# Attention kernel: the two transposed pieces of a cell back to back, and a step's fill in two parts

## The chip, the cores and the metric

The kernel runs on 1 core of a Trainium2 chip. The metric is device time in microseconds (us). The core's engines are TensorE (PE, its weight loads listed as PEld), VectorE (DVE), ScalarE (ACT), GpSimd (POOL) and SyncE (SP, which issues the DMAs). They run side by side and are ordered by semaphores that the program waits on and increments itself.

## What is computed

One transformer layer for x of shape (2, 1024, 512): attention with 32 query heads and 8 key/value heads of width 128, then a feed-forward layer with 4-bit weights, each with a residual and a layer norm. The part that matters here:

```python
scores = jnp.einsum('bhqd,bhkd->bhqk', q, k) * scale
scores = jnp.where(causal[None, None], scores, -1000000000.0)
attn = jax.nn.softmax(scores, axis=-1)
out = jnp.einsum('bhqk,bhkd->bhqd', attn, v)
out = out.transpose(0, 2, 1, 3).reshape(bsz, q_len, N_HEADS * HEAD_DIM)
return out @ Wo.T
```

Every product is made of three passes over operands that are split in a high and a low part (`PASSES`: high by high, high by low, low by high), so each logical 128x128 by 512 product is three matmuls of 512 columns.

## The kernel before

The program has three stages. A projects keys and values and stores them. B, the attention, takes about 1835 of the 2507 us. C is the feed-forward part. The change touches B alone.

B is a loop of 16 turns, one for each pair of batch and key/value head, of about 114 us each. A turn has 32 steps, one for each cell. Cell c is query tile i = c // 4 (128 queries) of head h = c % 4 in the group of four; its scores have 128 x (i + 1) columns, since the mask is causal. In step s:

- PE multiplies the scores of cell s into `b_sps` (three matmuls, or six from step 16 on), transposes cell s - 3 (`LAG`), and does some fill.
- DVE takes mask and maximum of cell s (L869) and writes it to SBUF (`b_sc`), and ACT makes the exponential of it (L708).
- DVE takes the reciprocal of the sum (L877) and ACT normalises (L714) for cell s - 2.
- The normalised cell s - 3 is transposed by PE in blocks of 128x128 (L1006) into PSUM, `b_tps`. ACT copies the high part of that to `b_pt` (L729, `hi_pt`), then DVE subtracts it for the low part (L887, `lo_pt`).

A cell's transposed blocks come in **pieces** of up to four: cells 0 to 15 have one piece, cells 16 to 31 two (the first has four blocks, the second one to four). There are two `b_tps` buffers, used in turn; from cell 16 on the first piece goes to one and the second to the other. A piece may be written when DVE has subtracted the piece two before it: `transposes` waits for `pt_lo`, beside the normalisation, `norm_done`.

**Fill** is the other work of PE in the turn: 24 jobs in the table FILL, with their earliest steps. They are the products with the values (`pv`), the output projection (`wo`) and the queries of coming steps (`q0`, `q1`), 300 matmuls of 512 columns a turn. Each job writes one of two banks, in turn, and may start when the job before it in that bank has been drained by ACT and DVE. ROOM says how many matmuls a step holds. `cut` divides the fill of a step among its places in the order, by SHARES: SHARES[1] for cells of one piece, SHARES[2] for two. Step 0 does all its fill ahead of its scores.

The order within a step is written by hand, for each engine. `part_of` divides the turn in four: steps 0 to 2, 3 to 15, 16 to 23 and 24 to 31. In steps 0 to 2 the transposed cells are 29, 30 and 31 of the turn before, which have two pieces. PE's orders are PE_ORDER; ACT's and DVE's (ACT_ORDER, DVE_ORDER) have "0" and "1" for the copies and subtractions of the two pieces. An engine works its instructions off in that order, so one that waits holds those behind it. If the shares are used up, a "fill" in the order does nothing:

```python
for job in PE_ORDER[part_of(step)]:
    ...
    elif job == "fill":
        if shares:
            fill(it, turn, shares.pop(0))
    elif job < len(ts):
        transposes(*cell, ts[job])
```

SP loads the keys of a turn at its step 0, after all scores of the turn before (`s_done`), and the other inputs far ahead.

Of the kernel before, what the change touches and what calls it, by code (L numbers as in the profile page):

```python
# [54 lines left out]
def pieces(c):  # L55

    i = c // GQ
    first = c if i < 4 else 16 + 2 * (c - 16)
    out = [(first, 0, min(4, i + 1))]
    if i >= 4:  # L60
        out.append((first + 1, 4, i - 3))
    return out
# [31 lines left out]
def part_of(step):  # L94

    return (step >= LAG) + (step >= 16) + (step >= 24)
# [12 lines left out]
             ("take", "max", "q", 0, 1))  # L109
PE_ORDER = (("scores", "fill", "fill", 0, "fill", 1),  # L110
            ("fill", "scores", 0, "fill", "fill", 1),
            ("scores", "fill", 0, "fill", 1, "fill"),
            ("scores", "fill", 0, "fill", 1, "fill"))

SHARES = ((1,), (0, 1), (1, 1.25, 1))


def products(kind, a):
# [50 lines left out]
def cut(parts, weights):  # L169

    total, shares = sum(b - a for _n, a, b in parts), []
    ends = [round(total * sum(weights[:k]) / sum(weights)) for k in range(len(weights) + 1)]
    for lo, hi in zip(ends, ends[1:]):
        at, share = 0, []
        for place, a, b in parts:
            x, y = max(lo, at), min(hi, at + b - a)
            if x < y:
                share.append((place, a + x - at, a + y - at))
            at += b - a
        shares.append(share)  # L180
    return shares
# [68 lines left out]
def attention(nc, x, xT, wqT, wkrT, wdkT, wupkT, wupvT, woT, cosT, sinT, xs_d, k_d, v_d, y_d):  # L250


    with ExitStack() as ctx:
# [700 lines left out]
        def _(pe):  # L954
# [126 lines left out]
            def turn_of(it, turn):  # L1081
                for step in range(CELLS):
# [5 lines left out]
                    ts = pieces(cell[1]) if cell else []  # L1088
                    shares = cut(parts, SHARES[len(ts)])
                    for job in PE_ORDER[part_of(step)]:  # L1090
# [560 lines left out]
```

## Time and profile before

| | |
|---|---|
| three runs | 2506.01, 2510.23, 2511.68 us; median 2510.23 |
| profiled execution | 2508.73 us, its span 2506.9 |
| DVE, ACT, POOL busy | 57%, 64%, 23% of the span |
| granted TensorE clock | 0.989 of full speed over the span |
| DMA queue q1 | 35.1% of 16 engines' span |

PE is the busiest engine by far, in every slice of the span after the first:

```profile
PE   6999999999999999999999999999999996899998
PEld 5887888888888888887888888888888875677876
DVE  3334666666656666665666666666666665842332
ACT  3223878787777877787777777787877762322211
```

Each digit is the busy share of a fortieth of the span in tenths. The attention loop is slices 4 to 33. A matmul's listed duration is longer than the distance to the next one, since they are pipelined: its end is modelled. So costs of PE's work are read here as distances between starts in the timeline.

### The profile page before, as it was taken

How to read it: one execution, taken by the hardware profiler on the slowest of the kernel's cores; microseconds unless marked ns; L12 is line 12 of the kernel's file. 1: busy time of each engine (PE TensorE's matmuls, PEld its weight loads, DVE VectorE, ACT ScalarE, POOL GpSimd, SP SyncE). 2: the span in 40 equal slices, each digit the busy share in tenths (PEclk: the TensorE clock that was granted, in tenths of full speed). 3: DMA queues.
4: the chain of work that ended last, by engine and by line, in shares of the span. 5: the costliest groups of instructions: out<-in, count | busy, mean ns of one | idle time of the engine just before them, and what ended most of it. 6: DMA issues, size and time to landing. Idle time of an engine off the chain costs nothing. (4 is left out here: it accounts for less than half of the span.)

```text
span 2506.9 us, 40455 instructions
## 1 busy us (share of the span) xinstructions
PE 2409.5 (96%) x12016; PEld 1996.6 (80%) x12016; DVE 1430.8 (57%) x3325; ACT 1598.3 (64%) x3204; POOL 573.1 (23%) x443
## 2 busy tenths in 40 slices
PE   6999999999999999999999999999999996899998
PEld 5887888888888888887888888888888875677876
DVE  3334666666656666665666666666666665842332
ACT  3223878787777877787777777787877762322211
POOL 4002323132231313132232313231322202300000
PEclk9999999999999999999999999999999998999999
DMA  8657333234242323233242423232332316520110
GB/s 292 225 209 287 123 100 116 95 106 129 80 161 90 126 84 126 100 109 113 93 155 69 152 79 130 90 123 92 109 125 84 122 39 185 155 75 34 50 34 17
DMA packets 109681, 293.33 MB, mean 117 GB/s; under 512 B 10689, under 2 KB 27585, under 8 KB 99969
## 3 DMA queue, kind: packets, MB, share of 16 engines
q1 hardware_dynamic: 109632, 292.73, 35.1%
q8 instruction: 25, 0.41, 0.1%
q14 instruction: 24, 0.19, 0.0%
HBM read 208.80 MB, written 88.08 MB: 118 GB/s over the span
## 5 line engine op out<-in xcount | busy, mean ns | idle before, releaser
L887 DVE TENSOR_TENSOR b_pt<-b_tps,b_pt 128x512 fp32r<-128x512 f32 (+3 forms) x768 | 427.5, 557 | 333.5 <-ACT b_pt L729 332.5
L714 ACT ACTIVATE b_sc<-b_sc,b_rinv 128x896 f32<-128x896 f32 (+7 forms) x512 | 397.3, 776 | 308.7 <-DVE b_rinv L877 303.6
L245 PE MATMUL b_sps<-b_kt,b_qs 128*128 128x512 f32 (+4 forms) x2304 | 501.6, 344 | 10.4 <-DMA b_kt<-k_d 10.4
L245 PE MATMUL b_ps<-b_pt,b_vt 128*128 128x512 f32 x1728 | 480.0, 404 | 2.5 <-DVE b_ys L898 2.5
L245 PE MATMUL b_ps<-b_xs,b_wq 128*128 128x512 f32 x1536 | 445.9, 410 | 16.9 <-DVE b_qf L851 13.2
L245 PEld LDWEIGHTS b_sps<-b_kt,b_qs 128*128 128x128 f32 x2304 | 404.1, 188 | 70.9 <-issue 16.5
L245 PE MATMUL b_ps<-b_wo,b_ot 128*128 128x512 f32 x1536 | 424.0, 406 | 1.8 <-DVE b_ys L898 0.6
L729 ACT ACTIVATE b_pt<-b_tps 128x512 fp32r<-128x512 f32 (+3 forms) x768 | 365.0, 475 | 64.1 <-PE b_tps L1006 63.4
L708 ACT ACTIVATE b_sc<-b_sc,b_nmax 128x896 f32<-128x896 f32 (+7 forms) x512 | 392.5, 767 | 1.0 <-DVE b_nmax L869 1.0
L869 DVE CUSTOM_DVE_ANT_0 b_sc<-b_sps,b_mask 128x896 f32<-128x896 f32 (+7 forms) x512 | 381.2, 745 | 0.6 <-issue 0.3
L1006 PE MATMUL b_tps<-b_ident,b_sc 128*128 128x128 f32 x2304 | 374.8, 273 | 2.4 <-DVE b_pt L887 1.6
L245 PEld LDWEIGHTS b_ps<-b_pt,b_vt 128*128 128x128 f32 x1728 | 310.8, 189 | 56.8 <-DVE b_ys L898 3.0
L1006 PEld LDWEIGHTS b_tps<-b_ident,b_sc 128*128 128x128 f32 x2304 | 289.9, 140 | 77.7 <-issue 8.3
L245 PEld LDWEIGHTS b_ps<-b_xs,b_wq 128*128 128x128 f32 x1536 | 272.4, 190 | 73.5 <-DVE b_qf L851 27.3
L245 PEld LDWEIGHTS b_ps<-b_wo,b_ot 128*128 128x128 f32 x1536 | 270.6, 189 | 48.6 <-DVE b_qf L851 4.1
L577 POOL TENSOR_TENSOR b_sw<-b_sw,b_sin 128x512 f32<-128x512 f32 x128 | 165.0, 1289 | 502.4 <-ACT b_sw L682 502.4
L581 POOL TENSOR_TENSOR b_qs<-b_qf,b_qs 128x512 fp32r<-128x512 f32 x124 | 160.4, 1294 | 480.9 <-ACT b_qs L688 480.9
L877 DVE RECIPROCAL b_rinv<-b_rsum 128x1 f32<-128x1 f32 x512 | 81.7, 160 | 246.6 <-PE b_sps L245 233.8
L245 PE MATMUL c_a<-c_xs,c_w 128*128 (+3 forms) x528 | 135.5, 407 | 8.2 <-DVE c_hb L1437 4.2
L1545 PE MATMUL c_y<-c_w,c_hs 128*128 128x512 f32 (+1 forms) x528 | 132.4, 400 | 7.1 <-DVE c_hs L1443 6.9
L590 POOL TENSOR_TENSOR b_wo<-b_wraw,b_wo 128x512 fp32r<-128x512 f32 x64 | 82.4, 1288 | 242.5 <-ACT b_wo L702 242.5
L851 DVE TENSOR_TENSOR b_qf<-b_ps,b_cos 128x512 f32<-128x512 f32 x128 | 88.5, 692 | 86.1 <-POOL b_qs L581 44.0
(127 smaller groups left out, 2315.1 us busy)
## 6 DMA issues: line engine op xcount, KB each, us to landing
b_xs<-xs_d SPq DMA_DIRECT2D x32, 2048.0 KB, 9.2
b_ys<-y_d SPq DMA_DIRECT2D x128, 256.0 KB, 2.6
y_d<-b_ys SPq DMA_DIRECT2D x128, 256.0 KB, 2.4
k_d<-a_ks SPq DMA_DIRECT2D x32, 512.0 KB, 4.1
v_d<-a_vs SPq DMA_DIRECT2D x32, 512.0 KB, 2.9
b_kt<-k_d SPq DMA_DIRECT2D x64, 256.0 KB, 4.5
b_vt<-v_d SPq DMA_DIRECT2D x16, 1024.0 KB, 4.8
b_wraw<-in_wqT SPq DMA_DIRECT2D x64, 256.0 KB, 2.7
```

The source lines that it names most:

```text
L245: ins = nc.tensor.matmul(out, *every[n], start=(n == 0), stop=(n == len(every) - 1))
L577: nc.gpsimd.tensor_tensor(sw[:], sw[:], sinq[:, blk * TB:blk * TB + TB], ALU.mult).then_inc(sin_done, 1)
L581: nc.gpsimd.tensor_tensor(qs[:, blk, h, LO], qf[:], qs[:, blk, h, HI], ALU.subtract).then_inc(q_lo, 1)
L590: nc.gpsimd.tensor_tensor(wo[:, h, LO], wraw[:, h % 2], wo[:, h, HI], ALU.subtract).then_inc(w_lo, 1)
L708: nc.scalar.activation(sc[:, slot, 0:w], sc[:, slot, 0:w], ACT.Exp, bias=nmax[:, slot:slot + 1], scale=-1.0, accum_out=rsum[:, slot:slot + ...
L714: nc.scalar.activation(sc[:, slot, 0:w], sc[:, slot, 0:w], ACT.Copy, scale=rinv[:, slot:slot + 1])\
L729: nc.scalar.activation(pt[:, u % PT_UNITS, HI, 0:nj, h * P:(h + 1) * P], tps[n % 2][:, 0:nj], ACT.Copy)\
L851: nc.vector.tensor_tensor(qf[:], bank[bk][:], cosq[:, blk * TB:blk * TB + TB], ALU.mult)\
L869: nc.vector.tensor_tensor_reduce(out=like_banks(sc[:, slot, 0:w], i), in0=both_banks(sps[c % 2], i), in1=like_banks(mask[:, S - w:S], i), ...
L887: nc.vector.tensor_tensor(pt[:, u, LO, 0:nj, h * P:(h + 1) * P], tps[n % 2][:, 0:nj], pt[:, u, HI, 0:nj, h * P:(h + 1) * P], ALU.subtract) ...
L1006: last = nc.tensor.transpose(tps[n % 2][:, j], sc[:, c % S_RING, (j0 + j) * P:(j0 + j + 1) * P], ident[:])
L1545: last = nc.tensor.matmul(yps[t][:], hs[0:w, f % 2, a, t * P:(t + 1) * P], w2[0:w, b, f], start=(f == 0 and k == 0), stop=(f == FT - 1 and ...
```

## The change

The third and fourth order of PE have both pieces of a cell next to each other, with one fill ahead of them and one behind. The fill of a step whose cell has two pieces is divided in two equal shares, where it was in three of 1 : 1.25 : 1.

```diff
@@ -109,10 +109,10 @@
              ("take", "max", "q", 0, 1))
 PE_ORDER = (("scores", "fill", "fill", 0, "fill", 1),
             ("fill", "scores", 0, "fill", "fill", 1),
-            ("scores", "fill", 0, "fill", 1, "fill"),
-            ("scores", "fill", 0, "fill", 1, "fill"))
-
-SHARES = ((1,), (0, 1), (1, 1.25, 1))
+            ("scores", "fill", 0, 1, "fill"),
+            ("scores", "fill", 0, 1, "fill"))
+
+SHARES = ((1,), (0, 1), (1, 1))
```

The orders of ACT and DVE stay, and so do FILL and ROOM: each step holds the same matmuls.

## Rows read from the trace of the kernel before

**Rows 1.** The page: span, and PE's busy time, its share, instructions

```profile
span 2506.9 us, 40455 instructions
...
PE 2409.5 (96%) x12016; PEld 1996.6 (80%) x12016; DVE 1430.8 (57%) x3325; ACT 1598.3 (64%) x3204; POOL 573.1 (23%) x443
```

**Rows 2.** Busy times by stretch: turn 8, then its steps 19 to 31

```profile
1146.22:1260.19 113.97, 112.30 (x590) 94.11 (x588) 71.58 (x176) 89.01 (x185) 30.70 (x24) 1.00 0.33 110
...
1205.19:1256.78 51.59, 51.59 (x273) 43.75 (x272) 33.53 (x72) 39.55 (x74) 10.38 (x9) 1.00 0.18 56
```

**Rows 3.** Groups of instructions: busy, mean ns, idle before, releaser

```profile
L1006 PE MATMUL b_tps<-b_ident,b_sc 128*128 128x128 f32 x2304 | 374.8, 273 | 2.4 <-DVE b_pt L887 1.6
```

**Rows 4.** PE's timeline in step 21 of turn 8: start, us, what

```profile
1212.02 1.09 PE L245 MATMUL b_ps<-b_pt,b_vt 128*128 128x512 f32 x4
1212.95 0.60 PE L1006 MATMUL b_tps<-b_ident,b_sc 128*128 128x128 f32 x4
1213.30 1.18 PE L245 MATMUL b_ps<-b_wo,b_ot 128*128 128x512 f32 x4
1214.32 0.27 PE L1006 MATMUL b_tps<-b_ident,b_sc 128*128 128x128 f32 x1
1214.34 1.17 PE L245 MATMUL b_ps<-b_wo,b_ot 128*128 128x512 f32 x4
```

**Rows 5.** PE's timeline, steps 0 to 4 of turn 8

```profile
1152.30 1.04 PE L1006 MATMUL b_tps<-b_ident,b_sc 128*128 128x128 f32 x8
1153.09 0.60 PE L245 MATMUL b_sps<-b_kt,b_qs 128*128 128x256 f32 x3
...
1155.27 0.60 PE L1006 MATMUL b_tps<-b_ident,b_sc 128*128 128x128 f32 x4
...
1156.52 0.60 PE L245 MATMUL b_sps<-b_kt,b_qs 128*128 128x256 f32 x3
1156.96 1.08 PE L245 MATMUL b_ps<-b_wo,b_ot 128*128 128x512 f32 x4
...
1158.34 0.60 PE L1006 MATMUL b_tps<-b_ident,b_sc 128*128 128x128 f32 x4
...
1159.47 0.60 PE L1006 MATMUL b_tps<-b_ident,b_sc 128*128 128x128 f32 x4
1159.83 0.60 PE L245 MATMUL b_sps<-b_kt,b_qs 128*128 128x256 f32 x3
1160.35 0.33 PE L1006 MATMUL b_tps<-b_ident,b_sc 128*128 128x128 f32 x1
1160.44 1.64 PE L245 MATMUL b_ps<-b_xs,b_wq 128*128 128x512 f32 x6
1161.92 0.52 PE L245 MATMUL b_sps<-b_kt,b_qs 128*128 128x256 f32 x3
```

**Rows 6.** Timelines of PE and DVE, steps 20 and 22 of turn 8

```profile
1209.04 0.60 PE L1006 MATMUL b_tps<-b_ident,b_sc 128*128 128x128 f32 x4
...
1216.41 1.09 PE L245 MATMUL b_ps<-b_wo,b_ot 128*128 128x512 f32 x4
...
1209.46 0.29 DVE L887 TENSOR_TENSOR b_pt<-b_tps,b_pt 128x128 fp32r<-128x128 f32 x1 [0.80 <-ACT b_pt L729]
...
1216.54 0.69 DVE L892 TENSOR_TENSOR b_ot<-b_ps,b_ot 128x512 fp32r<-128x512 f32 x1 [0.20 <-ACT b_ot L736]
```

**Rows 7.** ACT's timeline, steps 1 and 2 of turn 8

```profile
1155.90 0.60 ACT L729 ACTIVATE b_pt<-b_tps 128x512 fp32r<-128x512 f32 x1
...
1157.99 0.58 ACT L729 ACTIVATE b_pt<-b_tps 128x512 fp32r<-128x512 f32 x1
...
1158.98 0.60 ACT L729 ACTIVATE b_pt<-b_tps 128x512 fp32r<-128x512 f32 x1
```

**Rows 8.** DVE's timeline, step 2 of turn 8

```profile
1158.60 0.69 DVE L887 TENSOR_TENSOR b_pt<-b_tps,b_pt 128x512 fp32r<-128x512 f32 x1 [0.75 <-ACT b_pt L729]
...
1159.61 0.69 DVE L887 TENSOR_TENSOR b_pt<-b_tps,b_pt 128x512 fp32r<-128x512 f32 x1
```

**Rows 9.** Waits: who for whom, us in total, times, longest us

```profile
PE b_sps L245 <- DMA b_kt<-k_d: 10.4, 14, 1.6
```

## The prediction

> **What bounds the kernel now.** I read the page's busy times first: TensorE's matmuls are busy 96% of the span, DVE and ACT far less [rows 1]. Then the stage view, for one turn of the attention loop (1146.22 to 1260.19, turn 8 counted from 0) and for its steps 19 to 31. In the turn, matmuls are busy 112.30 of 113.97 us; in steps 19 to 31, busy and stretch are both 51.59 us [rows 2]. So PE sets the time, nothing is waited for in the steps that the change is named after, and 1.67 us a turn are lost elsewhere. In all 2304 transposes PE sat idle 2.4 us [rows 3]. Two questions are left: does PE work become cheaper when transposes are merged, and does the new order make PE wait? For the second I laid PE's timeline beside ACT's and DVE's and asked of each moved group what releases it and who waits for it.
>
> **What really changes.** PE_ORDER changes steps 16 to 31. In steps 16 to 18 the cell has one piece and SHARES[1] stands, so nothing moves. In steps 19 to 31, F T0 F T1 F becomes F T0 T1 F (F: fill, T0 and T1: the two pieces). But SHARES[2] is also used by steps 1 and 2, where the last cells (30 and 31) of the turn before are transposed in the order scores, fill, fill, T0, fill, T1. With two shares the third fill is empty: all fill now runs ahead of T0. Step 0 has no fill left by then; steps 3 to 15 have one piece. No instruction is added or removed on any engine, and no queue of SP or POOL is reordered.
>
> **Term 1, merging in steps 19 to 31.** Take step 21 [rows 4]. Four fills ahead of T0 take 0.93 us (0.2325 each). T0's four transposes take 0.35 to the start of the next fill, and the four fills behind them 1.02, 0.09 more than 0.93. So a group of four costs 0.35 + 0.09 = 0.44, or 0.11 each. The lone T1 behind them starts 0.02 ahead of the next fill and leaves the same tail, 0.11 again. The only run of eight, at step 0, takes 0.79 before the next matmul starts [rows 5], 0.44 more than the run of four: again 0.11 each. Cost is proportional to the count, whatever the grouping. I take zero. Rounding allows 0.02 us either way for each of 13 x 16 = 208 merges: -4 to +4 us.
>
> **Term 2, waits in steps 19 to 31.** T0 moves behind half the fill, up to three matmuls (0.7 us) later, and T1 up to two matmuls earlier, less T0's own shift. T1 needs its PSUM buffer drained by DVE (L887) for the cell before. The tightest is step 20: T0 moves from 1209.04 to about 1209.50 (two fills), T1 to 1209.94 behind it (0.44 for four); DVE frees the buffer at 1209.46 + 0.29 = 1209.75 [rows 6]. It passes by 0.19. Fill jobs that now start before T0 need their bank: in step 22 the query job would start at about 1216.41 + 0.93 = 1217.34, and its bank is drained at 1216.54 + 0.69 = 1217.23 [rows 6], passing by 0.11. Both cost zero; if such a wait does open by 0.2 us in both, it is 0.4 x 16 = 6 us. ACT gets T0 later, but steps 19 to 31 show no PE wait [rows 2], and what ACT makes in a step (the next cell's normalised scores) PE reads in the next step at the earliest.
>
> **Term 3, steps 1 and 2: the loss.** Here ACT and DVE run right behind PE. Today T0 of cell 31 starts at 1158.34 and ends 0.60 later at 1158.94 [rows 5]; ACT's copy starts at 1158.98 [rows 7]; it ends at 1158.98 + 0.60 = 1159.58 and DVE starts at 1159.61, ending at 1160.30 [rows 8]; the one transpose of step 3, which writes the same buffer, starts at 1160.35, and its lead of 0.09 to the next matmul is not that of an unwaited one (0.02) [rows 4, 5]. Its natural start: in step 2 three scores matmuls behind a group of transposes take 0.44 (1156.52 to 1156.96) [rows 5], so 1159.83 + 0.44 = 1160.27. The chain through ACT and DVE already ends last, by 0.08.
> The change puts three more fills ahead of T0 of cell 31: 3 x 0.23 = 0.69, so it starts at 1159.03, if nothing else holds it. ACT then copies at 1159.67, DVE subtracts 1160.30 to 1160.99, and step 3's transpose starts at 1161.04 instead of 1160.35: PE is 0.69 us late.
> Is another path later? In step 1 two fills move ahead of T0 of cell 30, which starts 0.46 later (1155.73, end 1156.33). ACT's copy at 1155.90 [rows 7] started as soon as T0 was there (1155.27 + 0.60), so it moves to 1156.36, and with it ACT's queue behind it: rope's hi part, the normalisation of cell 31, the copy of T1 of cell 30 (1157.99 to 1158.45 [rows 7]), exp. DVE's subtraction for that T1 moves from 1158.60 to 1159.06 and ends at 1159.75 [rows 8]. T1 of cell 31, which needs that buffer, would start at 1159.03 + 0.44 = 1159.47, its place of today [rows 5]; it waits until 1159.80, 0.33 late. That makes step 2 longer by 0.33 to 0.4 and step 3 by the rest: 0.69 is the total, not added to it. ACT is free for T0's copy at 1158.98 + 0.46 = 1159.44, before 1159.67. What ACT and DVE do behind that moves by some 0.4, less than PE, so by step 4 nothing new is late.
> Nothing gives the 0.69 back. PE waits 10.4 us in all for keys [rows 9] at the starts of turns, but that load is issued on the last scores of the turn (s_done), so it moves with PE. What PE waits for in steps 3 to 15 otherwise are drains of a bank (L851 and its like), chains that start at PE's own last matmul of a job and move with it.
> Turns 1 to 15 have such a step 2 and 3: 15 x 0.69 = 10.35. The tail after turn 15 has T0 and T1 without scores; I estimate 0.3 for it, between nothing and one more 0.69. Sum: +10.65 us, with 0 from terms 1 and 2.
> Per-turn bounds: 0.46, if T0 of cell 31 were moved only by what step 1's shift gives, to 0.77, if today's 0.08 of wait came on top. That is +7 to +12 us.
>
> **The time.** The profiled execution took 2508.73 us, of which its span is 2506.9 [rows 1], 1.50 below the median of the runs, 2510.23. Against itself it becomes 2519.4; against the median 2520.9, which I predict.
>
> **The rivals.**
> (a) The forecast: 2520.9, own range 2516 to 2525 (term 3's bounds give 2517 to 2522.5, and some of term 1's come on top). Chance 0.74.
> (b) Slower still: the passes of 0.19 and 0.11 in steps 20 and 22 turn into waits, since ACT's copies of T0 come late and DVE's later work with them, or the merged run costs 0.02 each: +10.65 + 6 = 2527, to 2531 with +4. For: the margins are thin. Against: the copies that free these buffers are released by DVE's maxima today, not by T0. Chance 0.08.
> (c) No change: PE's loss at steps 2 and 3 is given back at the keys' wait of the next turn. 10.4 us over 14 waits is 0.74 each [rows 9], just enough for 0.69. It decides if the load is not on PE's own path; the net is then +0.3, 2510.5. Against: the code's wait on the last scores. Chance 0.12.
> (d) Faster: merged transposes come closer. If the 0.08 to 0.09 behind a group is paid once per step rather than twice, at no longer pitch within, 208 x 0.085 = 17.7 us go: 2510.2 + 10.65 - 17.7 = 2503.2. It needs that a longer run hides its weight loads better; the run of eight at 0.44 for its second four speaks against. Chance 0.06.
> The Trainium skill, "TensorE: Matmul & The Clock Gate", section "Back-to-back issue gap", has a rule on the side of (d): pairs of weight load and matmul of 128 columns sustain about 81 ns each. By it, a run of eight would be near 0.65 us, an estimate; the trace has 0.79 for its starts alone, so here it does not hold, and by it alone the merged runs of 80 transposes a turn would gain an estimated 0.028 us each, 36 us in all. The sum goes by the rows.
>
> **How the numbers follow.** 0.2% (5 us) is about what a measurement of this kernel can tell from no change. Faster by more: (d), 0.06. Within: (c) and a thin lower edge of (a), 0.13. Slower: 0.81. The range for 8 in 10 leaves out (c), (d) and the upper half of (b): 2514.5 to 2527.
>
> **What would show it.** Step 2 of a turn (3.31 us from its scores, 1156.52, to the next, 1159.83 [rows 5]) longer by 0.3 to 0.4; step 3 (1159.83 to 1161.92, 2.09 [rows 5]) longer by 0.3; a PE wait on DVE L887 of some 0.3 to 0.5 us twice a turn, where all turns together have 1.6 now [rows 3]; steps 19 to 31 still 51.6 us, all busy. It is wrong if the step 3 transpose is not behind DVE's subtraction, or if steps 19 to 31 change by over 0.2 us.

## The result

The changed kernel takes 2521.18 us (median of 5 runs, 2517.47 to 2523.64), the kernel before 2507.12 (5 runs, 2504.60 to 2511.68). The ratio is 1.0052, 95% interval 1.0040 to 1.0065: slower by 13 us, between 10 and 16. The forecast was 10.65 us slower, at 2520.9. That the two absolute times lie 0.3 us apart is luck: the forecast stood on a median of 2510.23 us for the kernel before, and with more runs that median is 3.1 us lower.

The first line of the changed kernel's page, to set against [rows 1]:

```profile
span 2520.8 us, 40455 instructions
```

The instructions are the same in number; the span is 13.9 us longer, and matmuls are busy 96% of it as before. Not all of that belongs to the change. Here are the scores' matmuls, the kernel before first, then the changed one: count, ns of one, first and last start.

```profile
L245 PE MATMUL b_sps<-b_kt,b_qs x2304: 274/338/477, 241.3 to 2048.0; 128*128 128x384 f32 x48, 128*128 128x512 f32 x48, 128*128 128x256 f32 x32, 128*128 128x320 f32 x32
```

```profile
L245 PE MATMUL b_sps<-b_kt,b_qs x2304: 274/339/478, 242.8 to 2061.2; 128*128 128x384 f32 x48, 128*128 128x512 f32 x48, 128*128 128x256 f32 x32, 128*128 128x320 f32 x32
```

The attention loop starts 1.5 us later, in a stage that the change doesn't touch. From its first scores to its last it takes 1806.7 us before and 1818.4 after: 11.7 us more. That is the part to explain.

The waits of PE for DVE's subtraction, in all: us, times, longest. It was 1.6 us on the matmuls before [rows 3].

```profile
PEld b_tps L1006 <- DVE b_pt L887: 11.8, 28, 0.5
...
PE b_tps L1006 <- DVE b_pt L887: 8.9, 36, 0.7
```

A weight load stands ahead of each matmul and can show the same wait, so the two lines are not to be added.

**Steps 2 and 3.** PE's timeline of turn 8, from the scores of step 2 to those of step 4. It answers to [rows 5].

```profile
1163.36 0.60 PE L245 MATMUL b_sps<-b_kt,b_qs 128*128 128x256 f32 x3
1163.79 1.09 PE L245 MATMUL b_ps<-b_wo,b_ot 128*128 128x512 f32 x4
1164.72 1.31 PE L245 MATMUL b_ps<-b_xs,b_wq 128*128 128x512 f32 x5
1165.87 0.60 PE L1006 MATMUL b_tps<-b_ident,b_sc 128*128 128x128 f32 x4
1166.62 0.66 PE L1006 MATMUL b_tps<-b_ident,b_sc 128*128 128x128 f32 x4 [0.15 <-DVE b_pt L887]
1167.04 0.60 PE L245 MATMUL b_sps<-b_kt,b_qs 128*128 128x256 f32 x3
1167.88 0.33 PE L1006 MATMUL b_tps<-b_ident,b_sc 128*128 128x128 f32 x1 [0.25 <-DVE b_pt L887]
...
1169.44 0.52 PE L245 MATMUL b_sps<-b_kt,b_qs 128*128 128x256 f32 x3
```

Step 2, counted from its scores to the next, takes 1167.04 - 1163.36 = 3.68 us, where it took 3.31; step 3 takes 2.40, where it took 2.09. Turns 1 to 14 all show this, at 0.66 to 0.70 us for the two together. All nine fills stand ahead of the first piece, and the second piece starts 0.75 after it, not 0.44. ACT's and DVE's timelines of the same stretch tell why (ACT first; these answer to [rows 7, 8]):

```profile
1163.20 0.60 ACT L729 ACTIVATE b_pt<-b_tps 128x512 fp32r<-128x512 f32 x1 [0.44 <-PE b_tps L1006]
...
1166.50 0.60 ACT L729 ACTIVATE b_pt<-b_tps 128x512 fp32r<-128x512 f32 x1 [0.28 <-PE b_tps L1006]
```

```profile
1165.87 0.69 DVE L887 TENSOR_TENSOR b_pt<-b_tps,b_pt 128x512 fp32r<-128x512 f32 x1 [1.19 <-ACT b_pt L729]
...
1167.13 1.50 DVE L887 TENSOR_TENSOR b_pt<-b_tps,b_pt 128x512 fp32r<-128x512 f32 x2 [0.30 <-ACT b_pt L729]
```

ACT waits for the late first pieces of cells 30 and 31 (0.44 and 0.28). DVE's subtraction for the second piece of cell 30 ends at 1165.87 + 0.69 = 1166.56, and PE goes on at 1166.62. DVE's next subtraction starts at 1167.13 and takes about 0.7 of the two listed together: it ends near 1167.82, and step 3's transpose starts at 1167.88.

**Step 22.** It takes 4.61 us, where it took 4.40. The busy times of the step, the kernel before first, then the changed one:

```profile
1215.35:1219.75 4.40, 4.40 (x25) 3.77 (x24) 2.92 (x7) 3.57 (x9) 0.00 (x0) 1.00 0.00 0
```

```profile
1222.94:1227.55 4.61, 4.61 (x25) 3.74 (x23) 2.88 (x7) 3.38 (x7) 0.00 (x0) 1.00 0.00 0
```

PE's timeline in the changed kernel, then the query job's weight loads, then DVE's drain of the bank (the matmuls and the drain answer to [rows 6]):

```profile
1224.01 1.08 PE L245 MATMUL b_ps<-b_wo,b_ot 128*128 128x512 f32 x4
1225.05 0.72 PE L245 MATMUL b_ps<-b_xs,b_wq 128*128 128x512 f32 x2
```

```profile
1225.04 0.30 PEld L245 LDWEIGHTS b_ps<-b_xs,b_wq 128*128 128x128 f32 x2 [0.38 <-issue]
```

```profile
1224.11 0.69 DVE L892 TENSOR_TENSOR b_ot<-b_ps,b_ot 128x512 fp32r<-128x512 f32 x1 [0.20 <-ACT b_ot L736]
```

The query job's first matmul starts 1.04 us after the start of the four projections, not 0.93, and its second 0.33 after it, not 0.23. The group has 0.1 + 0.1 too much. Load and matmul start together, at 1225.04 and 1225.05. The bank was free at 1224.11 + 0.69 = 1224.80.

Turn 0 of the same kernel shows the job without the loss. DVE's drain, the job's loads, its matmuls:

```profile
305.61 0.69 DVE L892 TENSOR_TENSOR b_ot<-b_ps,b_ot 128x512 fp32r<-128x512 f32 x1 [0.20 <-ACT b_ot L736]
```

```profile
306.41 0.41 PEld L245 LDWEIGHTS b_ps<-b_xs,b_wq 128*128 128x128 f32 x2
```

```profile
306.64 0.62 PE L245 MATMUL b_ps<-b_xs,b_wq 128*128 128x512 f32 x2
```

There the drain ends 0.2 us earlier in the step, at 306.30, the load leads its matmul by 0.23, and step 22 takes 4.39. So in turn 8 the unhindered load would stand at about 1224.01 + 0.93 - 0.23 = 1224.71, and the drain is 0.09 late for it. The load then follows the drain by 0.24 (0.23 to 0.24 in each of turns 1 to 14), where the transposes of step 2 followed DVE's subtraction by 0.06. The profile puts the wait down to no engine (`issue`). The code of a query job (`queries`) has three waits in a row ahead of its first matmul, the bank's first, and the trace has instructions of PE's sequencer between the drain and the load. That these waits make up the 0.24 is likely, and not shown by a run.

**The rest.** The stretch that [rows 2] calls steps 19 to 31 ends where the scores of step 31 begin, so it holds steps 19 to 30; step 31 takes 3.41 us in both kernels, all of it busy. The busy times of steps 19 to 30 of turn 8, and of steps 24 to 30, in the changed kernel, after stretch and length:

```profile
1212.76:1264.45 51.69, 51.69 (x274) 44.25 (x272) 33.47 (x72) 39.54 (x72) 10.41 (x9) 1.00 0.18 56
...
1231.35:1264.45 33.10, 33.10 (x173) 28.16 (x171) 21.98 (x45) 26.04 (x46) 7.67 (x6) 1.00 0.12 40
```

Steps 19 to 30 go from 51.59 to 51.69 us [rows 2] though step 22 alone is 0.21 longer: steps 24 to 30 became shorter, 33.24 to 33.10. Turns 0 to 14 all show this 0.15. In turn 15, which has no queries of a next turn among its fill, the same steps are 0.71 us longer: the second piece now waits for DVE's subtraction in steps 25 and 28, 0.40 and 0.37 us, where it waited for nothing before. The view calls the whole stretch busy in both kernels; a wait of this kind between two matmuls is hidden under the modelled end of the one before.

### The profile page after: what moved, and what is told of

It reads as the page before. It is cut to its first block and busy times, and to the rows that moved or that the text cites. A ratio compares the mean times of both kernels' runs of the same rounds, so it can differ in the third digit from the quotient of the medians.

```text
span 2520.8 us, 40455 instructions
## 1 busy us (share of the span) xinstructions
PE 2415.6 (96%) x12016; PEld 2005.6 (80%) x12016; DVE 1428.4 (57%) x3325; ACT 1604.0 (64%) x3204; POOL 573.8 (23%) x443
## 5 line engine op out<-in xcount | busy, mean ns | idle before, releaser
L245 PE MATMUL b_sps<-b_kt,b_qs 128*128 128x512 f32 (+4 forms) x2304 | 501.4, 344 | 10.7 <-DMA b_kt<-k_d 10.7
L245 PE MATMUL b_ps<-b_pt,b_vt 128*128 128x512 f32 x1728 | 460.6, 399 | 2.1 <-DVE b_ys L898 2.0
L245 PE MATMUL b_ps<-b_xs,b_wq 128*128 128x512 f32 x1536 | 429.7, 406 | 16.3 <-DVE b_qf L851 13.2
L245 PE MATMUL b_ps<-b_wo,b_ot 128*128 128x512 f32 x1536 | 413.9, 403 | 1.3
L1006 PE MATMUL b_tps<-b_ident,b_sc 128*128 128x128 f32 x2304 | 340.8, 273 | 9.8 <-DVE b_pt L887 8.9
L1006 PEld LDWEIGHTS b_tps<-b_ident,b_sc 128*128 128x128 f32 x2304 | 277.7, 140 | 65.2 <-DVE b_pt L887 11.8
```

Source lines behind the costliest of these rows:

```text
L245: ins = nc.tensor.matmul(out, *every[n], start=(n == 0), stop=(n == len(every) - 1))
L1006: last = nc.tensor.transpose(tps[n % 2][:, j], sc[:, c % S_RING, (j0 + j) * P:(j0 + j + 1) * P], ident[:])
```

## The experiments

Each is the kernel before, or the changed one, with one part done or undone. All but the last read the shares of a step from a table:

```diff
+SHARES_AT = {...}
-                    shares = cut(parts, SHARES[len(ts)])
+                    shares = cut(parts, SHARES_AT.get(step, SHARES[2]) if len(ts) == 2 else SHARES[len(ts)])
```

with SHARES[2] at (1, 1.25, 1) again. Lines behind it are one higher than in the kernel before. My theory (A) was that the loss lies in steps 2 and 3 and in the bank wait of step 22, and that merging costs nothing. The rival (B) was that the merged order itself costs.

### Late steps alone

```diff
-            ("scores", "fill", 0, "fill", 1, "fill"),
-            ("scores", "fill", 0, "fill", 1, "fill"))
+            ("scores", "fill", 0, 1, "fill"),
+            ("scores", "fill", 0, 1, "fill"))
+SHARES_AT = dict.fromkeys(range(16, 32), (1, 1))
```

> The changed order and two shares in steps 16 to 31 alone; steps 1 and 2 of a turn keep their three shares. Theory A (the loss sits in steps 2 and 3, 0.68 us a turn, and in the bank wait of step 22, 0.22 us a turn; merging itself costs nothing): steps 2 and 3 back at 3.31 and 2.09 us, step 22 still at 4.61, and with the small differences of the other steps about 0.13 us a turn over the kernel before, +2 us in all (ratio 1.0008). Rival B (the merged order bears the loss, and steps 2 and 3 are late only because ACT's and DVE's work of steps 22 to 31 is): steps 2 and 3 stay long, +8 us or more (1.003 and up).

Measured: 2509.39 us against 2507.61, ratio 1.0007 (0.9999 to 1.0016). Its busy times from the scores of step 2 to those of step 4, and of step 22:

```profile
1157.69:1163.10 5.41, 5.41 (x34) 4.53 (x32) 4.15 (x14) 4.68 (x12) 1.30 (x1) 1.00 0.00 0
1216.60:1221.21 4.61, 4.61 (x25) 3.75 (x24) 2.89 (x7) 3.39 (x7) 0.00 (x0) 1.00 0.00 0
```

Steps 2 and 3 are back at 5.41 together (5.40 before), step 22 stays at 4.61. B falls: what the change does in the steps that it is named after bears some 2 of the 13 us, with an interval from nothing to 4.

### Early steps alone

```diff
+SHARES_AT = {1: (1, 1), 2: (1, 1)}
```

> The old order of steps 16 to 31 with three shares; only steps 1 and 2 have two shares, so all their fill stands ahead of the first piece. Theory A: step 2 3.68 us, step 3 2.40 us, all else as in the kernel before: 15 x 0.68 = +10.3 us (ratio 1.0041). Rival B: steps 2 and 3 hardly longer, at most +3 us.

Measured: 2520.94 us against 2507.61, ratio 1.0048 (1.0036 to 1.0060). The point, 12 us, is above the 10.3 of A, and 10.3 lies in the interval. PE's timeline in steps 2 and 3:

```profile
1164.81 0.66 PE L1007 MATMUL b_tps<-b_ident,b_sc 128*128 128x128 f32 x4 [0.16 <-DVE b_pt L888]
...
1166.07 0.33 PE L1007 MATMUL b_tps<-b_ident,b_sc 128*128 128x128 f32 x1 [0.25 <-DVE b_pt L888]
```

The same two waits, with the old order in all late steps. Nearly all of the loss comes from the shares, in steps whose order the diff doesn't show.

### Step 22 mended

```diff
 # late_only, and:
+SHARES_AT[22] = (4, 8)
```

> As late_only, but step 22 has 4 of its 12 fill matmuls ahead of the merged transposes and 8 behind, so that the query job starts behind them. Theory A (its bank is drained too late for the weight load of a first matmul that stands ahead of the transposes): step 22 falls from 4.61 to 4.38 to 4.40 us, and the whole to 0.09 us a turn under the kernel before, -1.5 us (ratio 0.9994). Rival C (step 22 is longer because the transposes or ACT's copies are late there, not for the bank): step 22 stays at 4.5 us or above.

Measured: 2506.21 us against 2507.61, ratio 0.9996 (0.9988 to 1.0005). Its step 22, busy times, and the transposes and queries in its timeline:

```profile
1214.27:1218.66 4.39, 4.39 (x25) 3.82 (x24) 2.90 (x7) 3.56 (x9) 0.00 (x0) 1.00 0.00 0
```

```profile
1216.26 0.71 PE L1007 MATMUL b_tps<-b_ident,b_sc 128*128 128x128 f32 x5
1216.73 2.09 PE L246 MATMUL b_ps<-b_xs,b_wq 128*128 128x512 f32 x8
```

4.39, with the transposes as merged as before. But they also stand two fills earlier, so this run alone doesn't exclude C, late transposes. The place of the loss does: in the changed kernel the time is lost ahead of the transposes, between the projections and the queries. This kernel has the lowest median of all, but its interval holds 1: it is not shown to be faster than the kernel before.

### One query matmul ahead

```diff
 # late_only, and:
+SHARES_AT[22] = (5, 7)
```

> As late_22, but with 5 of the 12 fills of step 22 ahead of the merged transposes: the fifth is the first matmul of the query job. Theory A (its wait for the drained bank stands ahead of its weight load, so it must be over a matmul's length before the start to cost nothing): step 22 long again, 4.60 us. Rival G (in the changed kernel the wait is caused by the transposes that follow, or by two query matmuls ahead of them): 4.4 to 4.5 us.

```profile
1216.92 1.08 PE L246 MATMUL b_ps<-b_wo,b_ot 128*128 128x512 f32 x4
1217.96 0.49 PE L246 MATMUL b_ps<-b_xs,b_wq 128*128 128x512 f32 x1
1218.29 0.71 PE L1007 MATMUL b_tps<-b_ident,b_sc 128*128 128x128 f32 x5
```

Step 22 took 1215.86 to 1220.44, 4.58 us, in a run of 2508.20. The first query matmul comes 1.04 after the start of the projections again, and 0.33 passes after it. One matmul ahead costs nearly what two cost: G falls, and the price hangs on where the job starts.

### Step 1 alone

```diff
+SHARES_AT = {1: (1, 1)}
```

> The kernel before with two shares in step 1 alone: the first piece of cell 30 comes two fills (0.46 us) later, step 2 keeps three shares. Theory A, worked through ACT's queue (copy of that piece 0.46 late, all behind it too, so the second piece of cell 31 and the transpose of step 3 wait for DVE's subtractions): steps 2 and 3 together longer by 0.35 to 0.46 us. Rival D (only the move of cell 31's own first piece counts, since ACT has slack in step 1): under 0.1 us.

One run of 2512.34 us. PE's timeline in steps 2 and 3:

```profile
1157.76 0.60 PE L246 MATMUL b_sps<-b_kt,b_qs 128*128 128x256 f32 x3
...
1159.89 0.65 PE L1007 MATMUL b_tps<-b_ident,b_sc 128*128 128x128 f32 x4 [0.15 <-ACT b_sc L715]
...
1161.44 0.60 PE L246 MATMUL b_sps<-b_kt,b_qs 128*128 128x256 f32 x3
```

Step 2 takes 3.68, 0.37 more, and step 3 what it took: its transpose starts 0.51 after the scores. The size is in my bounds and D falls, but the place is not the one that I named: it is the first piece of cell 31 that waits, and for ACT's normalisation (L715), not for DVE's subtraction. ACT's queue was late, as worked out, and the first thing that PE needs of it is that cell.

### Step 2 alone, in three sizes

```diff
+SHARES_AT = {2: (1, 1)}      # step2_only: 9 fills ahead of the first piece
+SHARES_AT = {2: (3, 5, 1)}   # step2_eight: 8
+SHARES_AT = {2: (3, 2, 4)}   # step2_five: 5, where the kernel before has 6
```

> The kernel before with two shares in step 2 alone: all 9 fills ahead of cell 31's first piece, where 6 were. Theory A (that piece, ACT's copy, DVE's subtraction and the transpose of step 3 are one chain without slack): steps 2 and 3 together +0.6 to +0.7 us a turn, all of it in step 3, since the second piece of cell 31 isn't held up (step 1 is as before). Rival E (the 0.31 us that the changed kernel loses in step 3 is all that step 2's move can cost, the 0.37 of step 2 being apart): +0.31 us in step 3.

> The kernel before with step 2's fill cut 3, 5, 1: 8 fills ahead of cell 31's first piece. Theory A: two fills later, 2 x 0.23 = 0.46 us more in step 3 and nothing in step 2. Rival F (step 3 has slack for a part of it): 0.2 us or less.

> The kernel before with step 2's fill cut 3, 2, 4: 5 fills ahead of cell 31's first piece, one fewer. Theory A: a chain of ACT's queue is then the later one (ACT comes free 0.04 us before its copy starts today), so steps 2 and 3 gain at most 0.05 us. Rival F: they gain the 0.08 us by which the transpose of step 3 waits today, or with each fill taken away 0.23 us.

The transpose of step 3 with the scores ahead of it, for nine fills and then for eight:

```profile
1164.56 0.60 PE L246 MATMUL b_sps<-b_kt,b_qs 128*128 128x256 f32 x3
1165.78 0.33 PE L1007 MATMUL b_tps<-b_ident,b_sc 128*128 128x128 f32 x1 [0.63 <-DVE b_pt L888]
```

```profile
1162.63 0.60 PE L246 MATMUL b_sps<-b_kt,b_qs 128*128 128x256 f32 x3
1163.62 0.33 PE L1007 MATMUL b_tps<-b_ident,b_sc 128*128 128x128 f32 x1 [0.39 <-DVE b_pt L888]
```

From those scores to the transpose: 0.52 us in the kernel before [rows 5], 0.99 with two fills more, 1.22 with three. That is +0.47 and +0.70, at 0.23 a fill, all in step 3. A is met; E and F fall. The runs took 2515.74 and 2517.87 us beside one of 2507.04.

With five fills:

```profile
1158.14 0.60 PE L246 MATMUL b_sps<-b_kt,b_qs 128*128 128x256 f32 x3
...
1159.83 0.65 PE L1007 MATMUL b_tps<-b_ident,b_sc 128*128 128x128 f32 x4
...
1161.60 0.60 PE L246 MATMUL b_sps<-b_kt,b_qs 128*128 128x256 f32 x3
1162.04 0.27 PE L1007 MATMUL b_tps<-b_ident,b_sc 128*128 128x128 f32 x1
```

Step 3's transpose follows its scores at the natural 0.44, and the next scores start at 1163.54, so step 3 falls to 1.94. But step 2 rises to 3.46: the first piece starts 1.69 after the scores, not 1.82, though a fill of 0.23 is gone, and what stands behind it is stretched. It waits for the normalisation of its own cell, as in `step1_only`:

```profile
1158.57 1.14 ACT L715 ACTIVATE b_sc<-b_sc,b_rinv 128x1024 f32<-128x1024 f32 x1
```

That ends at 1159.71, and the piece starts at 1159.83. Together 5.40, no gain, and step 4 is 0.07 longer; the run took 2509.55. So six fills stands between the two limits: with eight, step 3 is late, with five, step 2. Seven wasn't run.

### Where the small gain of steps 24 to 30 comes from

The fourth order and two shares alone, in steps 24 to 31:

```diff
             ("scores", "fill", 0, "fill", 1, "fill"),
-            ("scores", "fill", 0, "fill", 1, "fill"))
+            ("scores", "fill", 0, 1, "fill"))
+SHARES_AT = dict.fromkeys(range(24, 32), (1, 1))
```

> The changed order and two shares in steps 24 to 31 alone; steps 1, 2 and 19 to 23 as in the kernel before. Theory A: neither the chain of steps 2 and 3 nor the bank wait of step 22 is there, and the 0.16 us a turn that steps 24 to 31 gave back in the changed kernel is all that is left: -0.16 x 16 = -2.6 us (ratio 0.9990). Rival H (those gains came from PE being later than ACT and DVE after the stall in step 22): steps 24 to 31 as long as before, ratio 1.000.

Measured: 2506.53 us against 2508.32, ratio 0.9994 (0.9985 to 1.0003). Steps 24 to 30 of turn 8, in this kernel and in the kernel before:

```profile
1224.03:1257.12 33.09, 33.09 (x172) 28.18 (x171) 21.89 (x45) 25.96 (x46) 7.67 (x6) 1.00 0.11 40
```

```profile
1223.54:1256.78 33.24, 33.24 (x172) 27.85 (x171) 21.96 (x45) 26.16 (x48) 7.67 (x6) 1.00 0.12 39
```

0.15 us less, without the stall of step 22: H falls. The whole time moved the forecast way, by less than its interval can tell.

The merged order in step 26 alone, and one idle wait more at step 24:

```diff
-                    for job in PE_ORDER[part_of(step)]:
+                    for job in (("scores", "fill", 0, 1, "fill") if step == 26 else PE_ORDER[part_of(step)]):
+SHARES_AT = {26: (1, 1)}
```

> The kernel before with the changed order and two shares in step 26 alone, the step that became 0.05 us shorter. If a step's gain comes from its own merging: step 26 4.62 to 4.63 us against 4.675, its neighbours unchanged. If it comes from where the steps ahead of it put ACT's and DVE's work: step 26 within 0.01 us of 4.675.

```diff
+                    if step == 24:
+                        pe.wait_ge(masked, 4)
```

> The kernel before with one more wait on PE at the start of step 24, on a semaphore that has long been there (the mask's), so that nothing is waited for. If the distance between PE's matmuls depends on where instructions stand in PE's stream and not on work beside them, single steps from 24 on change by 0.01 to 0.05 us either way, though the work and its order are the same. If not, all steps stay within 0.005 us.

Step 26 took 1230.53 to 1235.19 = 4.66 us in the first (2507.00) and 1233.16 to 1237.84 = 4.68 in the second (2507.90), against 4.67 before and 4.62 in the changed kernel. So the gain of step 26 is not from its own merging, and the wait that waits for nothing changed no step from 24 to 30 by more than 0.02 us in turns 0 to 14. The six fills ahead of the transposes show where it lies, in `merge_26` and then in `last_part`:

```profile
1231.75 1.56 PE L246 MATMUL b_ps<-b_pt,b_vt 128*128 128x512 f32 x6
1233.15 0.82 PE L1007 MATMUL b_tps<-b_ident,b_sc 128*128 128x128 f32 x6
```

```profile
1234.29 1.53 PE L246 MATMUL b_ps<-b_pt,b_vt 128*128 128x512 f32 x6
1235.66 0.82 PE L1007 MATMUL b_tps<-b_ident,b_sc 128*128 128x128 f32 x6
```

The same six matmuls take 1.40 us in one (1231.75 to 1233.15) and 1.37 in the other, 0.233 or 0.228 each. What sets that distance is open.

## Why the prediction was right, and where it was not

**What changes.** Right, and it decided the case: two shares also move the pieces of steps 1 and 2. `early_only` and `late_only` divide the loss as 12 to 2 us.

**Term 1, merging costs nothing.** Right as far as a measurement of the whole can tell. Steps 24 to 30 gain about 0.15 us a turn in turns 0 to 14, 2.2 us in all, inside the 4 us that I allowed for rounding but not for that reason.

**Term 2, step 20.** Right: no wait came. But I read the margins of all steps from turn 8. In turn 15 two waits for DVE's subtraction opened, in steps 25 and 28, 0.7 us together and once, which the term had at nothing. The rows that I read as steps 19 to 31 hold steps 19 to 30; step 31 didn't change, so nothing hung on it.

**Term 2, step 22.** Wrong. I compared the bank's drain (1217.23) with the start of the matmul (1217.34) and called it a pass by 0.11. The wait stands ahead of the matmul's weight load, which leads it by 0.23 when nothing is in its way (turn 0). The load would have started at 1217.11, and the drain was 0.12 late for it; in the changed kernel it was 0.09 late. The load then comes 0.24 behind the drain, and the step pays 0.21 a turn. I had the case among the rivals, as (b), with 0.2 us for each such wait; it came in one of the two places. It came in 14 turns, 1 to 14, and over them is 3.1 us: turn 15 has no such job, and in turn 0 the drain ends in time.

**Term 3, steps 2 and 3.** Right in its size a turn: 0.37 + 0.31 = 0.68 against 0.69, as a maximum of two moves and not their sum. Step 1's move alone costs 0.37, step 2's alone 0.70, both together 0.68. The division between the steps (0.33 to 0.4, and the rest) came as worked out, and so did the waits: the weight loads of the two transposes stood idle for DVE's subtraction 28 times, 0.42 us each, twice in each of 14 turns. One link was wrong when step 1 moves alone: the normalisation of cell 31 is then the later one. In the changed kernel it is covered by the three fills. The lower bound of 0.46 named step 1's shift as a case; `step1_only` measures 0.37, so it should have been lower. I counted 15 turns. Turns 1 to 14 pay it. In turns 0 and 15 step 2 was long already, 5.99 and 3.94 us, and differs by 0.5 to 1.7 us among the kernels here, so that they tell little: over both, steps 2 and 3 are 0.5 us shorter in the changed kernel. The 0.3 for the tail can't be told either: the stretch from the last step's scores to the last products with the values differs by 2 us among these kernels.

**Nothing is given back.** Right: rival (c) needed the keys' wait to shrink. It was 10.4 us in 14 waits before [rows 9] and is 10.7 in 14.

**The sum.** Over all 16 turns, counted from scores to scores, steps 2 and 3 are 9.0 us longer (14 x 0.68 = 9.5, less the 0.5), step 22 is 3.1 longer, and steps 24 to 30 are 1.5 shorter (15 x 0.15, less the 0.7 of turn 15). That is 10.6; the loop lost 11.7, and the remaining 1.1 us lies in differences of single turns and of a few hundredths in other steps. The forecast's 10.65 had the first term alone, 10.35 of it for the loop. That was 1.3 too much there, and left out 3.1, -1.5 and 1.1, so the errors partly cancel and the sum came closer than its working deserved.

**Rival (d), and the rule of 81 ns.** Both fall. In step 22 of the mended kernel five transposes take 1216.73 - 1216.26 = 0.47 to the next fill, against 0.35 for four [rows 4], 0.12 more for one more: no closer than the 0.11 that I took. So a group of four and a lone one cost together what a group of five costs. The Trainium skill, "TensorE: Matmul & The Clock Gate", section "Back-to-back issue gap", says about 81 ns for such pairs; the trace disagrees, with eight in 0.79 [rows 5], 0.10 each.

## What to carry to other kernels

When a table is shared by several orders, list each place that reads it before you cost a change of it: here the steps that the change was not about took nearly all of the loss. Ask of each piece of work that moves later who is right behind it: 0.23 us of fill ahead of a transpose cost 0.23 us, since a copy, a subtraction and the next transpose hung on it without slack. Count a margin to the weight load ahead of a matmul, not to the matmul. And read it in the first and the last turn of a loop too: here one turn more had no wait in step 22, and one had two that no other had.

## What the runs showed of the hardware

A drain that ended 0.09 us too late for a weight load cost 0.21 us: the load came 0.24 behind the drain, the matmul was 0.11 late, and the next one 0.33 behind it instead of 0.23, since load and matmul had started together. The busy share doesn't show that: step 22 is 4.61 us busy of 4.61. And the mean distance of the same six matmuls of 512 columns in step 26 was 0.233 or 0.228 us by the kernel, with nothing waited for; no run here tells what decides it.
